# Gated cross-attention and feed-forward block on one core: the attention stage reordered on every engine, and the first norm's mean shift moved

## The reference, cut to what matters

```python
def layernorm(x): return (x - mean(x)) / sqrt(var(x) + 1e-5)          # over the last axis

def xattn(n, ctx, Wq, bq, Wk, bk):                                    # B=4, L=256, 128 context features
    q = ctx @ Wq.T + bq
    k = ctx @ Wk.T + bk
    attention = softmax(q @ k.T, axis=-1)                             # [B, 256, 256]
    return einsum('bln,bmn->blm', n, attention)

def ffn(n, w_gating, w_linear):                                       # operands rounded to fp8 e4m3
    return (gelu(n @ w_gating[0]) * (n @ w_gating[1])) @ w_linear     # 256 -> 1024 -> 256

x = x + tanh(g_xattn) * xattn(layernorm(x), ctx_1024, Wq, bq, Wk, bk) # x: [4, 256, 256] float32
x = x + tanh(g_ffn)   * ffn(layernorm(x), w_gating, w_linear)
```

## Time and profile before

| what | us |
|---|---|
| median of 3 runs (lowest, highest) | 50.71 (50.47, 51.29) |
| the profiled execution's own time | 50.60 |
| its span, as the profile shows it | 48.8 |
| first to last matmul of the attention stage, with its projections | 3.62 to 22.65 |
| first matmul of the feed-forward stage | 22.86 |

### The profile page before, as it was taken

One profiled execution on the slowest core, in us unless ns is written; L12 is line 12 of the kernel. 1 busy time (PEld: TensorE's weight loads), 2 busy tenths in 40 slices (PEclk: granted clock), 3 DMA queues, 4 the chain that ended last, 5 costly groups with the idle time before them and its releaser, 6 DMA issues.

```text
span 48.8 us, 842 instructions
## 1 busy us (share of the span) xinstructions
PE 42.2 (87%) x245; PEld 29.2 (60%) x245; DVE 35.7 (73%) x111; ACT 29.4 (60%) x67; POOL 16.9 (35%) x35
## 2 busy tenths in 40 slices
PE   0989999990999999998999999999999999995300
PEld 0318788860887988864435655766656788872000
DVE  2101059999978979989999991887666998899910
ACT  4601684399799599844599749754446944662000
POOL 3205992009999823410510160000000697005000
PEclk9999999999999999999999999999999999999965
DMA  0599999999999990000000000000000024400083
GB/s 0 81 320 153 336 378 309 186 203 196 199 199 139 105 95 4 0 0 7 0 13 0 0 0 0 0 0 0 7 0 0 0 104 164 168 8 0 0 322 108
DMA packets 3460, 4.64 MB, mean 95 GB/s; under 512 B 384, under 2 KB 2048, under 8 KB 3456
## 3 DMA queue, kind: packets, MB, share of 16 engines
q1 hardware_dynamic: 2592, 3.80, 24.6%
q0 software_dynamic: 864, 0.79, 17.3%
HBM read 5.90 MB, written 1.05 MB: 142 GB/s over the span
## 4 chain that ended last, share of the span: by engine, by line
PE 64%; DVE 15%; DMA 9%; SPq 3%; ACT 2%; issue 1%; DVEq 1%
PE bank L627 15%; PE bank L633 14%; PE bank L652 14%; PE bank L587 14%; DMA x_sb<-x 9%; DVE st L403 6%; PE bank L559 4%; SPq L206 3%; DVE nmax L410 2%; PE bank L609 2%; PE bank L552 2%; DVE mv L406 2%; DVE aq L470 2%; DVE attn L421 1%; ACT xq L337 1%
## 5 line engine op out<-in xcount | busy, mean ns | idle before, releaser
L461 DVE SCALAR_TENSOR_TENSOR ap<-bank,gl 128x512 f16<-128x512 f32 (+1 forms) x20 | 11.6, 581 | 3.5 <-issue 1.6
L346 ACT ACTIVATE gl<-bank 128x512 bf16<-128x512 f32 (+1 forms) x20 | 10.0, 508 | 6.0 <-PE bank L627 6.0
L652 PE MATMUL bank<-wl,aq 128*128 128x256 fp8e4 x64 | 10.1, 273 | 0.7 <-DVE aq L470 0.6
L627 PE MATMUL bank<-xq,wg 128*128 128x512 fp8e4 (+1 forms) x40 | 10.2, 337 | 0.2 <-ACT xq L337 0.2
L633 PE MATMUL bank<-xq,wg 128*128 128x512 fp8e4 (+1 forms) x40 | 10.2, 337 | 0.0
L652 PEld LDWEIGHTS bank<-wl,aq 128*128 128x128 f16 x64 | 6.0, 98 | 4.1 <-DVE aq L470 1.6
L587 PE MATMUL bank<-attnT,xT_sb 128*128 128x256 f32 x32 | 8.1, 385 | 0.0
L470 DVE TENSOR_SCALAR aq<-ap 128x512 uint16<-128x512 uint16 (+1 forms) x20 | 6.6, 334 | 0.0
L276 POOL TENSOR_TENSOR yo<-ys,x 128x256 f32<-128x256 f32 x4 | 2.9, 748 | 9.3 <-ACT ys L354 9.3
L587 PEld LDWEIGHTS bank<-attnT,xT_sb 128*128 128x128 f32 x32 | 5.6, 190 | 0.7 <-ACT attnT L320 0.2
L261 POOL TENSOR_TENSOR r<-ve,neg_half 128x2 f32<-128x2 f32 x4 | 3.0, 760 | 8.4 <-DVE ve L444 8.4
(11 more groups left out here) (51 smaller groups left out, 55.7 us busy)
## 6 DMA issues: line engine op xcount, KB each, us to landing
x_sb<-x SPq DMA_DIRECT2D x4, 256.0 KB, 4.8
xT_sb<-xT SPq DMA_DIRECT2D x4, 256.0 KB, 8.4
out<-yo SPq DMA_DIRECT2D x6, 128.0 KB, 2.0
wg<-w_gating POOLq DMA_DIRECT2D x4, 128.0 KB, 9.1
par<-params_ctxT SPq DMA_DIRECT2D x1, 258.0 KB, 2.8
par<-params_ctxT SPq DMA_DIRECT2D x1, 256.0 KB, 4.0
wl<-w_linear POOLq DMA_DIRECT2D x2, 128.0 KB, 11.7
out<-yo SPq DMA_DIRECT2D x1, 256.0 KB, 2.0
```

The source lines that it names most:

```text
L346: nc.scalar.activation(gl[:, s % 2, toks], gate_b[s % 2][:, toks], ACT.Gelu_apprx_tanh).then_inc(gelu_ready, 1)
L461: nc.vector.scalar_tensor_tensor(ap[:, s % NAP, toks], up_b[s % 2][:, toks], ACT_SCALE, gl[:, s % 2, toks], ALU.mult, ALU.mult).then_inc(p ...
L627: mm = nc.tensor.matmul(gate_b[s % 2][:, toks], wg8[:, c, k, 0, o:o + P], xq[:, g, k, toks], start=(k == 0), stop=(k == KC - 1))
L652: mm = nc.tensor.matmul(halves(y_b[g][i])[:, t], aq[:, s % NAQ, m:m + P], wl8[:, j], start=(j == 0 and t == 0), stop=(j == HT - 1), skip_g ...
```

## The change

1. **Loads.** The packed parameters are laid out anew and cut as: query weights, biases, gates, batch 0's context (388 columns) | key weights, batch 1's context (384 columns) | context of batches 2 and 3. SP issues the first and third cut, ACT the second. SP then issues x 0, x 1, xT 0, xT 1, x 2, xT 2, x 3, xT 3. POOL starts loading the gating weights after x 0 has landed, and the linear weights after its first normalising.
2. **Warm-up.** Six matmuls instead of five, on a constant of ones that exists already, so without the memset on DVE.
3. **First norm.** scales1 runs per pair of batches (h = 0 and 1, tiles 128x4 where they were 128x8), s1 first; nr1 and nms1 are made later (shifts1). add_attention adds x itself and not xs; shift_x is gone from POOL and ACT. POOL makes xr = x2 + nms1 (shift_residual) after rstd2, and the four last residual additions on POOL and DVE's finish read xr.
4. **Normalising.** POOL multiplies batches 1 and 3, DVE 0 and 2.
5. **Orders** of DVE, POOL, ACT and PE as in the diff. On PE, each attend follows its own turn directly.

```diff
@@ CUTS, loads @@
-    WARM_UP = 5
-    CTX_CUTS = ((0, 1), (1, 2), (2, 4))
+    WARM_UP = 6
+    CUTS = (0, P + 4 + L, NPAR + 2 * L, NPAR + 4 * L)
...
+            for c in (0, 2):
+                cols = slice(CUTS[c], CUTS[c + 1])
                 sp.dma_start(par[:, cols], params_ctxT[:, cols]).then_inc(s_ctx[c], 16)
...
+            load_x(0)
+            load_x(1)
+            load_xT(0)
+            load_xT(1)
+            load_x(2)
+            load_xT(2)
+            load_x(3)
+            load_xT(3)
@@ POOL @@
+            def scales1(h):
+
+                pool.wait_ge(mv1_ready, LT * GB * (h + 1))
+                nc.gpsimd.tensor_scalar(pair(ve1, h), pair(mv1, h)[:, :, :, 1], EPS, None, ALU.add).then_inc(ve1_ready, 1)
+                pool.wait_ge(ve1_ready, h + 1)
+                nc.gpsimd.tensor_tensor(pair(r1, h), pair(ve1, h), pair(neg_half, h), ALU.pow).then_inc(r1_ready, 1)
+                pool.wait_ge(r1_ready, h + 1)
                 pool.wait_ge(ntg_ready, 1)
...
+                nc.gpsimd.tensor_scalar(pair(s1, h), pair(r1, h), tg[:, 0:1], None, ALU.mult).then_inc(s1_ready, 1)
...
+            def shift_residual(b):
+
+                pool.wait_ge(nms1_ready, b // GB + 1)
+                pool.wait_ge(x2_ready, LT * (b + 1))
+                for t in range(LT):
+                    nc.gpsimd.tensor_scalar(xr[:, b, t], x2[:, b, t], 1.0, nms1[:, b, t:t + 1], ALU.mult,
+                                            ALU.add).then_inc(xr_ready, 1)
...
-            pool.wait_ge(s_ctx[1], 16)
+            pool.wait_ge(s_x[0], 16)
             for c in range(NWG):
                 load_w_gating(c)
+            pool.wait_ge(consts_ready, 1)
+            scales1(0)
+            normalise(1)
             for h in range(2):
                 load_w_linear(h)
-            pool.wait_ge(consts_ready, 1)
-            scales1()
-            shift_x(0)
-            shift_x(1)
-            normalise(B - 1)
-            for b in range(B):
-                rstd2(b)
+            normalise(3)
+            shifts1(0)
+            rstd2(0)
+            rstd2(1)
+            scales1(1)
+            shifts1(1)
+            rstd2(2)
+            shift_residual(0)
+            rstd2(3)
+            shift_residual(1)
+            shift_residual(2)
+            shift_residual(3)
@@ ACT @@
+            cols = slice(CUTS[1], CUTS[2])
+            act.dma_start(par[:, cols], params_ctxT[:, cols]).then_inc(s_ctx[1], 16)
...
             attn_out(1)
+
+            nc.scalar.activation(table[:, :], tg[:, 0:1], ACT.Gelu_apprx_tanh)
             attn_out(2)
-
-            nc.scalar.activation(table[:, :], tg[:, 0:1], ACT.Gelu_apprx_tanh)
-            shift_x(2)
             attn_out(3)
-            shift_x(3)
@@ DVE @@
             def add_attention(b):
                 dve.wait_ge(pv_done, b + 1)
-                dve.wait_ge(s1_ready, 1)
...
+                dve.wait_ge(s1_ready, b // GB + 1)
...
-            for b in range(B - 1):
-                stats1(b)
+            stats1(0)
             row_max(0)
-            stats1(B - 1)
+            stats1(1)
             row_max(1)
             normalise(0)
+            invert_sum(1)
             row_max(2)
-            normalise(1)
             row_max(3)
+            stats1(2)
             normalise(2)
-            invert_sum(B - 1)
+            invert_sum(3)
...
             norm2(0)
             norm2(1)
+            stats1(3)
             add_attention(2)
@@ PE @@
-            pe.wait_ge(idle_ready, 1)
+            ones = nc.const_aps.tensor(1.0, [P, TOK], BF16)
...
             energy(2)
             turn_attention(0)
             energy(3)
-            attend(0, [(0, 0), (0, 1)])
+            attend(0)
             turn_attention(1)
-            attend(0, [(1, 0), (1, 1)])
+            attend(1)
             turn_attention(2)
-            attend(1)
+            attend(2)
             turn_attention(3)
-            attend(2)
             attend(3, [(0, 0), (0, 1)])
             turn_x2(0)
             attend(3, [(1, 0)])
```

More of the change, by code:

```diff
@@ L73, in flamingo_block, with cT @@
         par = sb("par", [P, NPAR + B * L], F32)
[L74 to L77, removed]
+        wqT = par[:, 0:P]
+        bq, bk = par[:, P:P + 1], par[:, P + 1:P + 2]
+        gates = par[:, P + 2:P + 4]
+        wkT = par[:, P + 4 + L:P + 4 + L + P]
+        def cT(b):
+            o = P + 4 if b == 0 else NPAR + b * L
+            return par[:, o:o + L]
         x_sb = sb("x_sb", [P, B, LT, D], F32)
@@ L136, in flamingo_block @@
         x2_b = [bank[6], bank[1], bank[6], bank[7]]
-        s_ctx = [sem(f"s_ctx{c}") for c in range(len(CTX_CUTS))]
+        s_ctx = [sem(f"s_ctx{c}") for c in range(len(CUTS) - 1)]
         s_x = [sem(f"s_x{b}") for b in range(B)]
@@ L202, in _, with load_x, load_xT @@
         def _(sp):
-            for c, (b0, b1) in enumerate(CTX_CUTS):
-                cols = slice(NPAR + b0 * L if b0 else 0, NPAR + b1 * L)
+            for c in (0, 2):
+                cols = slice(CUTS[c], CUTS[c + 1])
                 sp.dma_start(par[:, cols], params_ctxT[:, cols]).then_inc(s_ctx[c], 16)
-            for b in range(B):
+            def load_x(b):
                 sp.dma_start(x_sb[:, b], x[b]).then_inc(s_x[b], 16)
-            for b in range(B):
+            def load_xT(b):
                 sp.dma_start(xT_sb[:, b], xT[b]).then_inc(s_xT[b], 16)
+            load_x(0)
[6 more added lines that the diff above has]
+            load_xT(3)
             for k in range(GB * LT):
@@ new lines, in pair @@
+            def pair(t, h):
+                return t[:, h * GB:(h + 1) * GB]
+            def scales1(h):
[4 more added lines that the diff above has]
+                pool.wait_ge(r1_ready, h + 1)
+                pool.wait_ge(ntg_ready, 1)
+                nc.gpsimd.tensor_scalar(pair(s1, h), pair(r1, h), tg[:, 0:1], None, ALU.mult).then_inc(s1_ready, 1)
@@ L275, in add_residual @@
                 pool.wait_ge(scaled_ready, b + 1)
-                nc.gpsimd.tensor_tensor(yo[:, b, t], ys[:, b, t], x2[:, b, t], ALU.add).then_inc(pool_y_ready, 1)
-            pool.wait_ge(s_ctx[1], 16)
+                pool.wait_ge(xr_ready, k + 1)
+                nc.gpsimd.tensor_tensor(yo[:, b, t], ys[:, b, t], xr[:, b, t], ALU.add).then_inc(pool_y_ready, 1)
+            pool.wait_ge(s_x[0], 16)
             for c in range(NWG):
                 load_w_gating(c)
+            pool.wait_ge(consts_ready, 1)
+            scales1(0)
+            normalise(1)
             for h in range(2):
                 load_w_linear(h)
-            pool.wait_ge(consts_ready, 1)
-            scales1()
-            shift_x(0)
-            shift_x(1)
-            normalise(B - 1)
-            for b in range(B):
-                rstd2(b)
+            normalise(3)
[10 more added lines that the diff above has]
+            shift_residual(3)
             for k in range(LT * GB):
@@ L320, in attn_out @@
                 nc.scalar.copy(attnT[:, b].rearrange("p k d -> p (k d)"), turn_b[b % 2][:, :]).then_inc(attnT_ready, 1)
[L322 to L326, removed]
             def norm2(b):
@@ L425, in add_attention @@
                 dve.wait_ge(pv_done, b + 1)
-                dve.wait_ge(s1_ready, 1)
[L427 to L430, removed]
+                dve.wait_ge(s1_ready, b // GB + 1)
                 for t in range(LT):
-                    nc.vector.scalar_tensor_tensor(x2[:, b, t], halves(pv_b[b % 2])[:, t], s1[:, b, t:t + 1], xs[:, b, t],
+                    nc.vector.scalar_tensor_tensor(x2[:, b, t], halves(pv_b[b % 2])[:, t], s1[:, b, t:t + 1], x_sb[:, b, t],
                                                    ALU.mult, ALU.add).then_inc(x2_ready, 1)
@@ L475, in finish @@
                 dve.wait_ge(ffn2_done, last_step(b) + 1)
+                dve.wait_ge(xr_ready, LT * (b + 1))
                 nc.vector.scalar_tensor_tensor(yo[:, b, t], halves(y_b[g][i])[:, t], yscale[:, 0:1],
-                                               x2[:, b, t], ALU.mult, ALU.add).then_inc(y_ready, 1)
-            nc.vector.memset(idle[:, :], 0.0).then_inc(idle_ready, 1)
+                                               xr[:, b, t], ALU.mult, ALU.add).then_inc(y_ready, 1)
             dve.wait_ge(ident_ready, 1)
@@ L528, in _ @@
         def _(pe):
-            pe.wait_ge(idle_ready, 1)
+            ones = nc.const_aps.tensor(1.0, [P, TOK], BF16)
             for i in range(WARM_UP):
-                nc.tensor.matmul(turn_b[0][:, :], idle[:, 0:P], idle[:, :], start=True, stop=True)
+                nc.tensor.matmul(turn_b[0][:, :], ones[:, 0:P], ones, start=True, stop=True)
             def project_q(b):
-                pe.wait_ge(s_ctx[min(b, len(CTX_CUTS) - 1)], 16)
+                if b != 1:
+                    pe.wait_ge(s_ctx[min(b, 2)], 16)
                 if b >= 2:
                     pe.wait_ge(q_ready, b - 1)
-                nc.tensor.matmul(q_b[b % 2][:, 0:L], wqT, cT[:, b * L:(b + 1) * L], start=True,
```

(5 more changed lines are left out.)

43 lines of the change are left out of this document (16 added, 27 removed).

## The result

The changed kernel takes 53.82 (median of 4 runs, 53.54 to 54.19) where the kernel before takes 50.94 beside it: the ratio is 1.059, with a 95% interval of 1.053 to 1.065. Slower was forecast, at 52.35 with a range up to 53.0; the time lies above the range. The profiled execution took 53.63, its span is 51.8 (before 50.60 and 48.8), so 3.0 us have to be found.

A forecast was written before the change was run, and what follows sets the result against it. PE was taken as the bound, after a start set by x 0's transfer and DVE. Profiled 50.60 + 1.87 (later up matmuls) - 0.15 + 0.05 = 52.37, said as 52.35; range 51.3 to 53.0.

The forecast's parts named there:

- T0: Start of PE's first attention turn (batch 0): 10.6 against 12.16 before, a gain of 1.56, range 10.3 to 11.0.
- from T0 to the end of attend 1: PE from the first turn to 16.68: attends of 1.73, and 0.87 of waiting for ACT's copy between turn and attend.
- add_attention(1) to stats1(3): On DVE, the same instructions between as before, so 3.51; batch 3's statistics start at 20.39.
- stats1(3) to add_attention(2): Batch 3's statistics on DVE, about 0.9, then a 2.1 wait for POOL's s1; add_attention(2) at 23.5.
- add_attention(2) to the third up group: DVE's 2.71 to the first product, then 0.73 to PE's up matmuls: 3.44, reaching 26.94.
- taken off, then added for the roundings: Feed-forward stage: 0.15 off for a shorter s1 and lead-in, 0.05 added for DVE's roundings beside POOL's shift_residual.
- the tail: The kernel's end: the same instructions as before, so nothing was added.
- The chain over POOL: After attend 1: batch 3's statistics, POOL's s1, add_attention(2), first product; PE's up matmuls come 1.87 later, stalling 1.1.
- Rival C: Feed-forward stage: DVE's rounding is slowed beside POOL's shift_residual, giving 52.9; chance 0.12.
- Rivals A and B: A: DVE's new wait is covered, 51.4 to 51.6, chance 0.17; B: turn-to-attend doesn't stop PE, 49.0 or 51.6, chance 0.06.
- The rival of late loads: At the start, xT 0 or batch 1's cut over 1 us late, so T0's gain goes: 53.5, chance 0.05.

The follow-up runs named there:

- n1: The kernel before with 21 more POOL instructions (memsets behind the last rstd2, nothing waits for them): 51.55, ratio 1.014.
- n2: The kernel before with 12 more POOL instructions (memsets behind the last rstd2, nothing waits for them): 51.37, ratio 1.011.
- e9: The changed kernel with only xr moved from POOL to ACT, between the gelus of steps 5 to 10: 52.72, ratio 1.036.
- e2: The changed kernel with batch 3's statistics directly behind invert_sum(3) on DVE and the second pair's scales1 ahead of rstd2(0) on POOL: 52.39, ratio 1.036.
- e3: The changed kernel with PE's old order and batch 3's statistics and the second pair's scales moved earlier: 49.98, ratio 0.990.
- e5: The changed kernel with PE's old order, early statistics and scales, and all parameter cuts issued by SP: 50.64, ratio 0.996.
- e1: The changed kernel with PE's old order, another piece of work between each turn and its attend: 53.84, ratio 1.050.

## Why the prediction was wrong

The mechanisms that it named were the ones the trace shows, and it had the direction right. One step failed outright: a term put at nothing. Beside it several sizes were off. In the profiled execution the change cost 3.03, where the sum had 1.77. The 1.26 between them are these:

| term of the sum | forecast | measured | off by |
|---|---|---|---|
| T0, the first turn | 10.60 | 10.83 | +0.23 |
| from T0 to the end of attend 1 | 6.08 | 6.24 | +0.16 |
| add_attention(1) to stats1(3) | 3.51 | 3.51 | 0 |
| stats1(3) to add_attention(2) | 3.11 | 2.93 | -0.18 |
| add_attention(2) to the third up group | 3.44 | 3.81 | +0.37 |
| taken off, then added for the roundings | -0.15, +0.05 | 0, 0 | +0.10 |
| the tail | 0 | 0.58 | +0.58 |

- **The tail, "the same instructions: nothing".** This is the step that failed. It was argued from the instructions and left out that the program itself is loaded while it runs. POOL's longer program brought one more such transfer, at the last outputs (n1, n2, e9), for 0.58 in the profile. With it alone the forecast would have been 52.9, still 0.7 short of the profiled 53.63; the terms below are that rest.
- **T0 = 10.6, by a landing at 3.45.** The landing was at 3.79 and T0 at 10.83: +0.23. The rule of the Trainium skill that the prediction put aside (DMA: Bandwidth & Descriptors, "Issuing engines are not separate DMA queues") was nearer: by it the landing was to be near 3.9 and T0 0.3 later. The clock was up at 5.45, 4.7 after the first warm-up matmul, and in the kernel before at 5.84, 4.7 after as well. The prediction had read 4.4, but the shift by 0.4 that it drew from it came.
- **From T0 to the end of attend 1.** Turn to attend was 1.28 (13.96 to 15.24), 0.84 of it waiting where 0.87 was priced. But an attend of a batch took 1.83 to the next turn in place of 1.73, and attend 0, for which PE did not stand idle but whose copy had also only just come (11.49 + 0.59 = 12.08, attend 0 at 12.16), took 1.80. The price of 1.73 came from attends whose operand had been ready. The page shows 0.68 for each wait, as it counts from the end of the turn's last matmul; the time lost on PE is 0.84.
- **The chain over POOL.** To the statistics it came as forecast. The next leg was shorter, as s1 took 0.30 and not 0.45, and the power 1.04 (1.09 by the straight line). That is the gain for which 0.15 had been taken off once more at the end. The last leg was longer by 0.37, and the stop ahead of add_attention(3) makes 0.35 of it (0.42 between two starts in place of 0.07). The profile puts its 0.26 of idle time down to "issue". All traces with the changed add_attention have the stop, except that in e2 a longer wait for PE stands in its place; the kernel before, n1 and n2 do not have it. Where it shows, an 8 KB transfer of instructions begins 0.65 to 0.68 after it ends. Whether the two belong together no run shows, and its cause stays open.
- **Rival C** did not come. Of the roundings two fell beside shift_residual, and took 0.38 and 0.28, not 0.83. The contention that the Trainium skill states in GPSIMD Engine Reference, section 8, "Key points", shows in these traces for POOL's additions with two inputs, and next to nothing of it for the shift with one, in these two cases.
- **Rivals A and B** did not come either: DVE's wait for s was 1.98 and not covered, and PE's three waits for the copies sum to 2.5.
- **The rival of late loads** had 53.5, the number nearest to the result, but not its reason: T0's gain came, 1.33 of it.

The predicted values were worked out from one execution, but the early part varies from one to the next: over the traces of this study the clock was up at 3.9 (e3) at the earliest and 7.4 (n1) at the latest, and x 0 landed between 5.5 (e9) and 8.2 (e5). A range of 0.3 to 0.4 about T0 was too narrow for a single profile.

What stays open beside the stop: what decides when x 0 lands, and whether the warm-up's length matters; neither was tried.

## What to carry to other kernels

When an order of work is changed on two engines, follow the chain to the first point where both meet, and price each wait with the other gone: here PE's waits of 2.5 us on the copies and of 1.0 us on the product were worth 2.88 us together, and 0.15 and 1.14 singly, between the first turn and the third up group. Before calling small work on an idle engine free, look at the end of the profile: here the longer program of an engine that had time cost a transfer of instructions where the last outputs were written. And when a kernel's variants are compared by one profile each, compare from a common event onwards, such as the first turn here, as the early part varies by itself.

## What the runs showed that was not expected

Twenty-one more instructions on POOL, for which nothing waits, lengthened the end by 0.58 us, with one transfer of 8 KB among the last output's packets; 12 did not. The granted clock fell to half after a wait of 3.19 in e1, and not after one of 1.15 in the kernel before or three of 0.84 in the changed one. And the clock was up from 3.86 in e3 and only from 5.45 in the changed kernel, whose PE programs are the same up to the first turn.
